# Attended rows of a sparse attention layer: written by VectorE to the partitions that the output product reads, in four copies for each pair of blocks

## What is computed

```python
_, idx = jax.lax.top_k(I, kk)                      # 96 keys for each token, 64 of them its local window
key_c = (c_kv @ W_uk)[bi, idx].reshape(B_, L_, kk, N_HEAD, D_HEAD)
value = (c_kv @ W_uv)[bi, idx].reshape(B_, L_, kk, N_HEAD, D_HEAD)
...
scores = (jnp.einsum('bhld,bhlkd->bhlk', q_c, k_c) + jnp.einsum('bhld,blkd->bhlk', q_r, key_r)) * scale
attn = jax.nn.softmax(scores.astype(jnp.float32), axis=-1).astype(v.dtype)
out = jnp.einsum('bhlk,bhlkd->bhld', attn, v)
out = out.transpose(0, 2, 1, 3).reshape(B_, L_, N_HEAD * D_HEAD)
return out @ W_out
```

## Time and profile before

| | us |
|---|---|
| median of 3 runs | 1689.7 (1689.04 to 1690.89) |
| the profiled execution | 1688.96 |
| its span, first to last instruction | 1686.8 |
| loop over the blocks | 703 to 1137 |
| last copies, mixing, additions | 1137 to 1156 |

### The profile page before, as it was taken

How to read it: one execution, slowest core, us unless ns; L and a number is a source line. 1 busy time by engine, 2 the same in 40 slices (tenths; PEclk the granted TensorE clock), 3 DMA queues, 4 the chain that set the end, 5 groups by cost and what they waited for, 6 DMA issues and landing times.

```text
span 1686.8 us, 31737 instructions
## 1 busy us (share of the span) xinstructions
PE 1401.3 (83%) x10664; PEld 915.3 (54%) x10664; DVE 1243.8 (74%) x2568; ACT 976.6 (58%) x1788; POOL 447.8 (27%) x751
## 2 busy tenths in 40 slices
PE   3599999799994754789999989996399999799994
PEld 2355554577773311456656655675255555577773
DVE  4578886698778577677878887754478887488787
ACT  2166666478883672346455555552166666488883
POOL 4122222100002023245455445622222233100000
PEclk9599999799997965899899999997599999799998
DMA  5211110022202244122122122212311110022200
GB/s 143 95 48 45 43 47 11 1 102 76 75 26 78 47 121 112 30 61 61 36 80 73 38 61 63 74 36 81 110 33 47 46 47 18 2 102 75 75 25 25
DMA packets 65020, 99.72 MB, mean 59 GB/s; under 512 B 21109, under 2 KB 44853, under 8 KB 62840
## 3 DMA queue, kind: packets, MB, share of 16 engines
q1 hardware_dynamic: 55254, 80.43, 15.5%
q0 software_dynamic: 8192, 16.79, 3.9%
q10 hardware_dynamic: 1440, 0.80, 0.2%
HBM read 73.39 MB, written 10.69 MB: 50 GB/s over the span
## 4 chain that ended last, share of the span: by engine, by line
PE 55%; DVE 13%; ACT 10%; DMA 6%; issue 6%; SPq 5%; DVEq 4%; ACTq 1%; POOL 0%; POOLq 0%
PE twin L973 8%; PE twin L963 5%; PE twin L827 5%; PE twin L1142 5%; PE twin L805 5%; DMA ffn<-arena 4%; PE twin L772 4%; ACT arena L1209 4%; DVEq L1830 2%; ACT experts L1279 2%; PE twin L1170 2%; PE twin L1158 2%; PE twin L1123 2%; PE twin L1186 2%; ACT arena L1277 2%
## 5 line engine op out<-in xcount | busy, mean ns | idle before, releaser
L1209 ACT ACTIVATE arena<-twin 128x1024 f32<-128x1024 f32 x288 | 293.8, 1024 | 172.7 <-PE twin L805 170.8
L750 POOL DMA_INDIRECT arena<-kv_rows,IDX x256 | 251.6, 983 | 309.9 <-PE twin L1189 151.0
L1478 DVE TENSOR_REDUCE arena<-twin 128x8 f32<-128x1024 f32 (+1 forms) x160 | 195.3, 1225 | 77.2 <-PE twin L772 42.9
L1277 ACT ACTIVATE arena<-twin,bias 128x512 f32<-128x512 f32 x256 | 184.9, 722 | 60.6 <-PE twin L963 60.6
L1527 DVE TENSOR_TENSOR experts<-arena,experts 128x512 fp32r<-128x512 f32 x256 | 170.1, 689 | 61.8 <-ACT experts L1279 60.5
L963 PE MATMUL twin<-experts,experts 128*128 128x512 f32 x768 | 197.0, 403 | 6.1 <-ACT experts L1279 6.1
L772 PE MATMUL twin<-ffn,ffn 64*128 64x128 f32 (+3 forms) x1152 | 154.8, 351 | 50.5 <-DMA arena<-arena 27.7
L1468 DVE TENSOR_REDUCE arena<-twin 128x2 f32<-128x1024 f32 x128 | 152.9, 1222 | 51.8 <-PE twin L772 48.4
L1279 ACT ACTIVATE experts<-twin,bias 128x512 fp32r<-128x512 f32 x256 | 186.2, 727 | 0.0
L973 PE MATMUL twin<-experts,experts 128*128 128x512 f32 x768 | 183.3, 390 | 1.0 <-DVE experts L1527 1.0
L711 POOL TENSOR_SCALAR_AFFINE_SELECT arena<-arena 128x256 f32<-128x256 f32 x256 | 99.6, 407 | 307.6 <-ACT arena L1209 307.6
(11 more groups left out here) (258 smaller groups left out, 2186.6 us busy)
## 6 DMA issues: line engine op xcount, KB each, us to landing
arena<-wt_rows SPq DMA_DIRECT2D x16, 1024.0 KB, 4.8
arena<-in_L_ffn_w SPq DMA_DIRECT2D x32, 256.0 KB, 5.2
ffn<-q_rows SPq DMA_DIRECT2D x64, 128.0 KB
ffn<-k_rows SPq DMA_DIRECT2D x64, 128.0 KB
XT<-idx_rows SPq DMA_DIRECT2D x16, 512.0 KB, 4.1
q_rows<-ffn SPq DMA_DIRECT2D x8, 512.0 KB, 4.9
k_rows<-ffn SPq DMA_DIRECT2D x4, 1024.0 KB, 9.2
arena<-HN SPq DMA_DIRECT2D x32, 128.0 KB, 2.4
```

Source lines behind the costliest of these rows:

```text
L750: pool.indirect_dma_start(G[d % GR][:, g, :], None, kv_rows, bass.IndirectOffsetOnAxis(ap=IDX[:, q, k * GB + g:k * GB + g + 1], axis=0))\
L1209: act.activation(PT[(UNITS * buf + u) % PT_RING].rearrange("p s n -> p (s n)"), twin[2 * u % S_RING][:, :], ACT.Exp, scale=float(HD) ** -0 ...
L1277: act.activation(H1[tb % 2][:, f, :], bank[f][:, :], ACT.Gelu_apprx_tanh, bias=bias1[buf][:, f:f + 1])
L1478: dve.tensor_reduce(to, scores.rearrange("p (s t k) -> p s t k", s=2, t=to.shape[2]), AX_X, ALU.max).then_inc(max_done, 1)
```

## The change

`dve_attended` writes straight to `OAX`. Each pair of blocks takes four copies, one for each partition group `r`: heads `r` and `r + 4`, 2 x 32 numbers in each of 32 partitions, read in runs of four tokens. `sp_moved`, the array `OA` and the semaphores `oa_moved` go, with SyncE's two waits for the index scores; TensorE's mixing waits for `oa_ready`, counted to 16 and 32 calls of `dve_attended`.

```diff
@@ -452,7 +451,6 @@
-        oa_moved = [sem(f"oa_moved{b}") for b in range(B)]
@@ -580,14 +578,6 @@
-        def sp_moved(sp, q):
-
-            sp.wait_ge(oa_ready, 4 * (q + 1))
-            for tile in (far_tile(q), near_tile(q)):
-                t = slice(tile * P, (tile + 1) * P)
-                for h in range(NH):
-                    sp.dma_start(OAX[h % 4 * DC:(h % 4 + 1) * DC, h // 4, t], OA[:, h, t]).then_inc(oa_moved[q // 4], 16)
-
@@ -624,19 +614,8 @@
-            for q in range(1, 4):
+            for q in range(1, PHASES):
                 sp_near(sp, q)
-            scored = [v for v in SCORED if INDEX[v][1] < PHASES]
-            sp.wait_ge(ix_done, scored[-1] + 1)
-            for q in range(3):
-                sp_moved(sp, q)
-            sp_near(sp, 4)
-            sp_moved(sp, 3)
-            for q in range(5, PHASES):
-                sp_near(sp, q)
-            sp.wait_ge(ix_done, SCORED[-1] + 1)
-            for q in range(4, PHASES):
-                sp_moved(sp, q)
@@ -1076,7 +1055,7 @@
                 if gq % (NG // B) == 0:
-                    pe.wait_ge(oa_moved[gq // (NG // B)], 16 * NH * TB)
+                    pe.wait_ge(oa_ready, NB // 4 // B * (gq // (NG // B) + 1))
@@ -1914,9 +1893,9 @@
-                cols = slice(pair * 2 * P, (pair + 1) * 2 * P)
-                m = dve.tensor_copy(OA[:, :, t0:t0 + 2 * BT].rearrange("p h (g t) -> p g h t", t=4),
-                                    o[:, cols].rearrange("p (g h t) -> p g h t", h=NH, t=4))
+                heads = o[:, pair * 2 * P:(pair + 1) * 2 * P].rearrange("p (g x r t) -> p r x g t", x=2, r=4, t=4)
+                for r in range(4):
+                    m = dve.tensor_copy(OAX[r * DC:(r + 1) * DC, :, t0:t0 + 2 * BT].rearrange("p x (g t) -> p x g t", t=4), heads[:, r])
             m.then_inc(oa_ready, 1)
```

More of the change, by code:

```diff
@@ L360, in build @@
         QALL = view("sel", (NH, TOK))
-        OA = QALL[0:DC]
         RAW = QALL.rearrange("p h t -> p (h t)")
```

## The result

The changed kernel took 1718.9 us (median of 4 runs, 1716.7 to 1722.2) against 1690.1 of the kernel before on the same chip (4 runs, 1689.0 to 1690.9): a ratio of 1.0173, 95% interval 1.0152 to 1.0193. It is 28.8 us slower where 16 were forecast. Its profiled execution took 1717.2 us with a span of 1715.0, which is 28.2 us over the span of before.

What follows compares the result with a forecast made beforehand. VectorE was taken to set the pace in the loop, though TensorE holds most of the chain; transfers bound only the tail. Terms 15.8 + 8.5 + 1.0 - 9.2 = 16.1 us more gave 1706 us, range 1696 to 1719.

Steps and rivals of the forecast that it cites:

- the clock in the loop: Block loop: more idle time lets TensorE's clock fall more often, costing 1 us, between nothing and 5.
- chain steps: Block loop: 14 attended steps on the chain of waits each pass their whole growth of 1.13 us, 15.8 us together.
- One attended step: VectorE: eight copies, none overlapping, take 1.89 us where two took 0.76, so a step grows by 1.13 us.
- Rival (a): Attended steps: the copies overlap, a step grows by 0.36 us, total -2.5 us, 1687 us; chance 0.08.
- The 17 other steps: Block loop: attended steps beside the chain of waits pass half a microsecond each, 8.5 us together.
- The tail: Behind the loop: the mixing's second half no longer waits for transfers and runs at full clock, gaining 9.2 us.
- Rival (c): Every step passes its growth whole and the tail's clock is no better: +31 us, 1721 us; chance 0.18.
- Rival (b): Steps in the loop mostly hide in slack, so the tail makes the kernel faster, down to 1680.5 us; chance 0.06.

Runs made afterwards that it cites:

- filled: The changed kernel with 16 extra TensorE products that nobody reads ahead of the transposes of every fourth block; 1709.1 us, 1.0111 of the kernel before.
- one_group: The changed kernel with all eight copies of a step written to partitions 0 to 31; 1694.1 us, 1.0030 of the kernel before.
- other_steps: two_copies with the eight copies only in the 17 steps off the chain of waits of the kernel before; 1696.7 us, 1.0044 of that kernel.
- filled_two: two_copies with 16 TensorE products that nobody reads ahead of the transposes of every fourth block; 1690.8 us, 1.0009 of the kernel before.
- two_copies: The changed kernel with the old two copies per attended step and no transfers; 1676.5 us, 0.9922 of the kernel before.
- chain_filled: chain_steps with 16 TensorE products that nobody reads ahead of the transposes of every fourth block; 1704.9 us, 1.0093 of the kernel before.
- chain_steps: two_copies with the eight copies only in the 14 steps on the chain of waits of the kernel before; 1712.3 us, 1.0129 of that kernel.
- the best kernel: The kernel before with direct copies in the last phase alone, plus 16 unread products behind the 14 steps on its chain; 1678.5 us, 0.9923 of it.

## Why the prediction was right in its sign and too small

The step that failed is the term for the clock in the loop: "I take 1 us, between nothing and 5". At least 9.3 us stand there (filled), and 15.1 are what the steps' own growth leaves unexplained. With it failed the bound on the chain steps, that each "moves the end by all it grows". The rest of the sum held within 2.5 us a term.

- **One attended step: right.** Forecast 1.89 us with copies of 211 ns; measured 1.79 to 1.92, mean 1.85, with 220 ns. Growth 1.10, not 1.13. The hold that it chose on the rows of L1785 and of the gap behind L1903 is shown by one_group. Rival (a) fell: 1.17 us is what overlap would have given, as it said (1.12).
- **The 17 other steps: right.** 8.5 us forecast. In the timelines of before and after their intervals grew by 11.0, 0.65 each, inside the 0.3 to 0.8 that it allowed; in other_steps they grew by 12.3. Reading the slack behind three of them gave the right size, a little low. That they "lie beside" the chain was true of before alone: in after the chain runs through 15 of the 17.
- **The tail: right.** 9.2 us forecast, 10.1 measured up to the last addition, with no idle time ahead of the second half and the clock at 1.00 in it. The products of the mixing took 11.8 us in their two pieces (5.47 and 6.29) and take 8.4 in one, 3.4 us less where 2.5 were forecast; the other 6.7 are the idle time, as forecast. The first half, too, came out faster, which the sum had left out. Behind the last addition came 1.6 us more that no step forecast; that stretch varies by more than this from kernel to kernel. The choice "the second half at full clock" was sound.
- **The 14 chain steps: too small.** The statement is "a piece of the chain that grows moves the end by all it grows: 14 x 1.13 = 15.8 us". The intervals behind them grew by 30.5 us, 2.2 each. A step's own growth is no upper bound: even at full clock in both kernels a step passed 1.26 us in the mean of the five intervals above (0.98 to 1.57), for a growth of 1.10, and beyond that comes the clock, next.
- **The clock in the loop: the term that failed.** "I take 1 us, between nothing and 5, since where VectorE leads a slower TensorE costs nothing." The loop's growth with its last interval is 41.5 us; 14 x 1.10 and the 11.0 of the others are 26.4, and 15.1 are left against the 1 us forecast. The reason given, that a slower TensorE costs nothing where VectorE leads, is what was wrong. In the interval behind step 12 the slower TensorE cost 2.57 us of 3.82. The timeline there shows how, read from one interval: VectorE leads up to the reciprocal; then TensorE starts late, on the path, at 1.2 GHz, and what it is late with is what the other engines wait for next.
- **Rival (c)** gave 1721, near the 1718.9 measured, but by another account: that all 31 steps pass whole, with 3 us for the clock, and the tail gives only 6.7. The others pass little more than half, the clock took far more, and the tail gave 10.1; that the numbers meet is luck. Rival (b) fell with the loop's growth of 40.2 us.

In sum, by the prediction's own terms: 15.8 + 8.5 + 1.0 - 9.2 became 15.4 + 11.0 + 15.1 - 11.7 and -1.5 ahead of the first step, 28.3 against the 28.2 of the spans.

**What stays open** is the exact split of the 15.1 us. filled gives 9.3 us back, and its products themselves take TensorE's time: in filled_two the loop grew by 4.5 us over two_copies although its time at 1.2 GHz fell by 31. So the clock's share is at least 9.3 us; how much of the rest is the clock's, and how much is that a step passes more than it grows, chain_filled was to tell and did not: its loop still had 31 us at 1.2 GHz. That its products were too short is read from one interval. Products sized to each wait would tell it; no such kernel was run. An estimate from single intervals: 2.57 us for the 6.8 at 1.2 GHz behind step 12 and 4.03 for 10.2 behind step 23 are 0.38 and 0.39 us for each, and at that price the 55 us more at 1.2 GHz would be 21 us. That is more than the 15.1, so the clock alone could be all of it, and it can't have cost this price everywhere. That the copies of the loop were delayed by memory or a queue was not seen in any row.

## What to carry to other kernels

Where an engine's queue feeds another through a short dependent chain (here copies, reciprocal, scaling, transposes), the length of the single piece ahead of the chain counts more than the engine's sum: 256 copies in pieces of 1.85 us cost the loop 39 us, the same 256 in pieces of 1.17 us cost 11 and in pieces of 0.35 us cost 8. And a chain read from one profile is no price list: once all steps had grown, it ran through twice as many of them. Before cutting one copy in four, look where the pieces go: if each writes another partition group than the one ahead of it, none overlaps. And take a transfer off only where the chain of waits has it; the last of eight phases held all of the gain that was found, and the direct copies that the other seven take in place of their transfers only cost.

## What the hardware showed that I had not expected

TensorE's clock fell behind short waits in a loop where it is otherwise nearly always busy: of the 14 stretches at 1.2 GHz in the loop of after, 13 begin in or just behind a wait of 1.3 to 3.2 us, and one behind two waits of 0.6 and 0.7. Not every such wait is followed by one: of the waits of 1.70 us in before and in two_copies, shown above, one was and one was not. And a fall outlasts the wait: behind the wait of 1.96 us above it worked at 1.2 GHz until about 913, and the interval had 6.8 us of it. The Trainium skill ("TensorE: Matmul & The Clock Gate", section "A second HAM failure mode: psum-queue depth-cycling") tells of a kernel whose clock swings when TensorE is idle for short times between groups of products; the trace agrees in that, with 89 us at 1.2 GHz where there were 34, though what makes TensorE idle here is another engine's work. This is the timeline of chain_steps (start, length, line, operation) with the one-hot products at 1.2 GHz and at 2.4:

```profile
721.70 4.42 PE L1122 MATMUL twin<-XN,arena 128*128 128x512 bf16 x11 [0.33 <-issue]
...
728.77 2.54 PE L1122 MATMUL twin<-XN,arena 128*128 128x512 bf16 x11
```

Sixteen products that nobody reads, some 1.07 us of work (33.1 us in filled's 31 places) behind 14 of the steps, go with the best kernel being 4.2 us faster than it was without them (1682.7 to 1678.5, and 4.4 us in the loop). The same products in each of the 31 steps, where the loop had few such waits, cost more than they gave: filled_two's loop is 4.5 us longer than two_copies'.
